# A decoder layer in five stages: loads and constants of each stage taken in the stage ahead, and the mixer's round in another order

## What is computed

```python
x = layernorm(x + mixer(x))                     # Mamba-2 block
x = layernorm(x + cross_attention(x, ctx, ctx)) # 16 heads of 64, softmax over 77 keys
x = layernorm(x + experts(x))                   # top 2 of 8, each with its own layernorm
```

## Time and profile before

| what | value |
|---|---|
| median of 3 runs | 2413.42 us |
| profiled execution, its own time | 2424.2 us |
| its span, first to last instruction | 2422.4 us |
| TensorE busy | 2166.8 us, 89% |
| VectorE busy | 1706.4 us, 70% |
| ScalarE busy | 1502.7 us, 62% |
| GpSimd busy | 1158.3 us, 48% |
| mean granted TensorE clock | 0.935 |

### The profile page before, as it was taken

How to read it: one execution, slowest core, us unless ns; L and a number is a source line. 1 busy time by engine, 2 the same in 40 slices (tenths; PEclk the granted TensorE clock), 3 DMA queues, 4 the chain that set the end, 5 groups by cost and what they waited for, 6 DMA issues and landing times. The chain is left out here.

```text
span 2422.4 us, 53619 instructions
## 1 busy us (share of the span) xinstructions
PE 2166.8 (89%) x15740; PEld 1925.9 (80%) x15741; DVE 1706.4 (70%) x4406; ACT 1502.7 (62%) x3174; POOL 1158.3 (48%) x1379
## 2 busy tenths in 40 slices
PE   5999999999995988999999999999949999999776
PEld 5888888878885977888888888888848998999633
DVE  5777777777775325677767767776738777777778
ACT  5777777777773426666666666666615565655433
POOL 2556556556553002334434434343336676766655
PEclk8999999999996999999999999999969999999955
DMA  4111111111101552232222223222167777777488
GB/s 145 32 35 35 35 35 35 35 35 35 35 30 39 188 189 73 89 105 79 82 91 78 82 78 95 77 82 90 52 193 222 230 237 229 232 237 228 144 294 266
DMA packets 185344, 278.70 MB, mean 115 GB/s; under 512 B 26092, under 2 KB 107508, under 8 KB 185268
## 3 DMA queue, kind: packets, MB, share of 16 engines
q1 hardware_dynamic: 171220, 241.04, 32.2%
q0 software_dynamic: 12960, 35.67, 4.1%
q10 hardware_dynamic: 1088, 1.07, 0.2%
HBM read 184.33 MB, written 93.38 MB: 115 GB/s over the span
## 5 line engine op out<-in xcount | busy, mean ns | idle before, releaser
L1499 ACT ACTIVATE b_wk_f<-b_ps_s,b_nmx 128x77 f32<-128x77 f32 x1024 | 233.7, 347 | 15.4 <-DVE b_nmx L1547 15.4
L599 DVE SCALAR_TENSOR_TENSOR a_conv<-a_xc_pad,a_cw,a_conv 128x256 f32<-128x256 f32 x384 | 217.9, 628 | 10.7 <-ACT a_conv L478 10.7
L1507 ACT ACTIVATE b_pT<-b_ps_pT 77x1024 f32<-77x1024 f32 x128 | 130.6, 1020 | 142.5 <-PE b_ps_pT L1405 142.5
L112 PE MATMUL c_ps_h<-c_xT_hi,c_w 128*128 128x256 f32 x568 | 168.0, 296 | 36.4 <-DMA c_b_c<-in_c_b 26.9
L2114 POOL DMA_INDIRECT made_scratch<-c_o_s,c_to x142 | 150.5, 1060 | 98.7 <-issue 40.5
L1986 ACT ACTIVATE c_hid<-c_ps_h,c_b_c 128x256 f32<-128x256 f32 x284 | 111.1, 474 | 119.7 <-issue 71.9
L1563 DVE TENSOR_TENSOR b_oT_lo<-b_ps_oT,b_oT_hi 128x512 fp32r<-128x512 f32 x128 | 88.0, 687 | 130.1 <-ACT b_oT_hi L1513 130.1
L1490 ACT ACTIVATE b_qT<-b_ps_q,b_bq_s 128x256 f32<-128x256 f32 x256 | 107.5, 472 | 113.2 <-PE b_ps_q L114 111.1
L1792 POOL CAST w<-b_w_raw 128x256 f32 (+1 forms) x32 | 13.6, 426 | 324.9 <-DMA b_w_raw<-in_c_w 324.9
L112 PE MATMUL c_ps_o<-w,c_h_hi 128*128 x568 | 161.3, 284 | 6.6 <-DVE c_h_lo L2030 6.6
L2030 DVE TENSOR_TENSOR c_h_lo<-c_hid,c_h_hi 128x1024 fp32r<-128x1024 f32 x71 | 98.0, 1380 | 97.9 <-ACT c_h_hi L1995 66.5
(11 more groups left out here) (286 smaller groups left out, 7822.5 us busy)
## 6 DMA issues: line engine op xcount, KB each, us to landing
c_w<-parts_scratch SPq DMA_DIRECT2D x71, 1024.0 KB
c_xa<-sent_scratch SPq DMA_DIRECT2D x71, 260.0 KB, 2.9
d_got<-made_scratch SPq DMA_DIRECT2D x32, 512.0 KB, 5.2
keys_scratch<-k_k_s SPq DMA_DIRECT2D x8, 1232.0 KB, 4.7
b_kz<-keys_scratch SPq DMA_DIRECT2D x64, 154.0 KB, 2.8
b_vv<-values_scratch SPq DMA_DIRECT2D x32, 308.0 KB
a_xT_f<-in_xT SPq DMA_DIRECT2D x32, 256.0 KB, 3.0
a_x_f<-in_x SPq DMA_DIRECT2D x32, 256.0 KB, 2.7
```

Of the source, the lines that this page charges most:

```text
L112: eng.matmul(out, lh, rh, start=start, stop=False)
L599: dve.scalar_tensor_tensor(out=conv[:, m, :], in0=xc_pad[:, m, k:k + L], scalar=cw[:, m, k:k + 1], in1=conv[:, m, :], op0=ALU.mult, op1=AL ...
L1499: last = act.activation(pe_[:, u.par, c, :], s_scores[:, c // (C // GM), c % (C // GM), :], ACT.Exp, bias=nmx[:, u.par, c:c + 1])
L1507: act.activation(pT[:, u.par, :, :], ps_pT[0:LK, :, :], ACT.Copy).then_inc(s_pTc, 1)
```

## The change

The mixer's lists are put in another order on four engines. On TensorE `turn_x` comes first, `cumulate` behind `turn_y`, `step_size` between the halves of `decay`, and `out` behind `in_z`. On ScalarE `take_x` and `x_high_next` stand ahead of `cum_high`, `take_bc` behind both exponentials and `squares` behind `silu_z`. On VectorE `normalise` stands first and the taps follow both `weigh` steps. On GpSimd `scale_x` stands ahead of `inv_rms`.

`prep_decay` and its waits move ahead of VectorE's rounds; the first `x_low` moves ahead of GpSimd's wait for the constants. The attention weights are loaded in round 1, together with the first context chunk, by a new `KeysHead`. The key weights are split in the mixer's last rounds (`keys_high`, `keys_low`). The mixer no longer waits for its last stores; the keys stage does, on ScalarE and SyncE. The context has one raw buffer instead of two. The keys stage loads attention's first x1 and keys for two items. To make room several tiles become views of others (the mixer's split weights lie in the key weights' place, `mk_pair` in `e_x`, `wo_stage` in `mt`, the attention stage's small tiles in `c_f`, `mk` and the split weights).

```diff
         w_stage = sb("w_stage", [P, KD, W_IN])
-        w_hi = sb("w_hi", [P, KD, C_DT], F32R)
-        w_lo = sb("w_lo", [P, KD, C_DT], F32R)
-        wo_stage = sb("wo_stage", [P, MI, D])
+        w_hi, w_lo = following.wk_hi, following.wk_lo
...
+            def load_following(b):
+                if b.known() and b.value() == 1:
+                    following.load(sp)
+
             load_xT(Item(0, 1))
-            following.load(sp)
-            run_steps(sp, n_seq, [(store, 3), (load_xT_ahead, 0), (load_x, 0)], spare=2)
-            for par in (0, 1):
-                sp.wait_ge(s_x1_out[par], 16 * (n_seq // 2))
+            run_steps(sp, n_seq, [(store, 3), (load_xT_ahead, 0), (load_x, 0), (load_following, 0)], spare=2)
...
             run_steps(pe, n_seq, [
-                (in_x, 0), (cumulate, 1), (turn_y, 2), (turn_x, 1), (in_bc, 0), (scores, 1), (decay(0), 1),
-                (out, 2), (decay(1), 1), (in_z, 0), (step_size, 0), (mix, 1), (mix_off, 1)])
+                (turn_x, 1), (in_x, 0), (turn_y, 2), (cumulate, 1), (in_bc, 0), (scores, 1), (decay(0), 1),
+                (step_size, 0), (decay(1), 1), (in_z, 0), (out, 2), (mix, 1), (mix_off, 1)])
...
             run_steps(act, n_seq, [
-                (cum_high, 1), (x_high_next, 0), (y_high, 2), (take_xc, 0), (take_bc, 0), (exp_rc, 1),
-                (exp_decay(0), 1), (take_x, 1), (squares, 2), (exp_decay(1), 1), (silu_z, 0), (silu_conv, 0),
+                (keys_high, 2), (x_high_next, 0), (take_x, 1), (cum_high, 1), (y_high, 2), (take_xc, 0), (exp_rc, 1),
+                (exp_decay(0), 1), (exp_decay(1), 1), (take_bc, 0), (silu_z, 0), (squares, 2), (silu_conv, 0),
                 (softplus, 0)], spare=2)
...
             run_steps(dve, n_seq, [
-                (cum_parts, 1), (y_low, 2), (mask_g, 1), (normalise, 3), (taps(0, 1), 0), (weigh(0), 1),
-                (taps(1, 2), 0), (weigh(1), 1), (taps(2, 3), 0), (bias_dt, 0), (add_d, 1), (prep_once, 0),
+                (keys_low, 2), (normalise, 3), (cum_parts, 1), (y_low, 2), (mask_g, 1), (taps(0, 1), 0), (weigh(0), 1),
+                (weigh(1), 1), (taps(1, 2), 0), (taps(2, 3), 0), (bias_dt, 0), (add_d, 1), (prep_once, 0),
                 (residual, 2), (log_decay, 0)], spare=2)
...
+            x_low(Item(0, 0))
             pool.wait_ge(s_load, 16 * N_LOADS)
             pool.wait_ge(s_pow, 4)
-            x_low(Item(0, 0))
...
             run_steps(pool, n_seq, [
-                (x_low_next, 0), (spread_cum, 1), (inv_rms, 2), (scale_x, 1), (join, 1), (inv_std, 2)], spare=2)
+                (x_low_next, 0), (spread_cum, 1), (scale_x, 1), (inv_rms, 2), (join, 1), (inv_std, 2)], spare=2)
...
+class KeysHead:
...
+    def load(self, sp):
+        self.weights.load(sp)
+        sp.dma_start(self.c_f[:, :, :], self.ctxT[:, :, 0:self.ROWS]).then_inc(self.s_c_in[0], 16)
+
+    def high(self, act):
+        act.wait_ge(self.weights.s_c, 16 * self.weights.CONSTANTS)
+        act.activation(self.wk_hi[:, :, 0:self.weights.DH], self.weights.wk_f[:, :, :], ACT.Copy).then_inc(self.s_khi, 1)
+
+    def low(self, dve):
+        dve.wait_ge(self.s_khi, 1)
+        dve.tensor_tensor(self.wk_lo[:, :, 0:self.weights.DH], self.weights.wk_f[:, :, :],
+                          self.wk_hi[:, :, 0:self.weights.DH].bitcast(F32), ALU.subtract).then_inc(self.s_klo, 1)
...
             def load_c(ch):
-                if ch >= 2:
-                    sp.wait_ge(s_chi, ch - 1)
-                    sp.wait_ge(s_clo, ch - 1)
-                sp.dma_start(c_f[:, ch % 2, :, :], ctxT[:, :, ROWS * ch:ROWS * ch + ROWS]).then_inc(s_c_in[ch % 2], 16)
+                sp.wait_ge(s_chi, ch)
+                sp.wait_ge(s_clo, ch)
+                sp.dma_start(c_f[:, :, :], head.ctxT[:, :, ROWS * ch:ROWS * ch + ROWS]
+                             ).then_inc(s_c_in[ch % 2], 16)
...
-            load_c(0)
             load_c(1)
             for ch in range(CHUNKS):
                 for sub in range(SUBS):
...
+                if ch == CHUNKS - 2:
+                    for par in (0, 1):
+                        sp.wait_ge(head.s_x1_out[par], 16 * (n_seq // 2))
+                    proj.load_xa(sp, x1)
+                    sp.wait_ge(s_ready, 2)
+                    sp.wait_ge(s_k_out[0], 16)
+                    proj.load_keys(sp, keys)
```

More of the change, by code:

```diff
@@ L941, in load, with __init__, sb @@
         sp.dma_start(self.mk[:, :, :], masks).then_inc(self.s_c, 16)
+class KeysHead:
+    ROWS = 8 * 77
+    def __init__(self, nc, ctx, signals, weights, ctxT):
+        def sb(name, shape, dt=F32):
+            return ctx.enter_context(nc.sbuf_tensor("k_" + name, shape, dt))
+        self.weights, self.ctxT = weights, ctxT
+        self.wk_hi = sb("wk_hi", [P, KD, 1152], F32R)
+        self.wk_lo = sb("wk_lo", [P, KD, 1152], F32R)
+        self.c_f = sb("c_f0", [P, KD, self.ROWS])
+        self.s_c_in, self.s_x1_out = ([signals.take(f"k_{n}{i}") for i in range(2)] for n in ("c_in", "x1_out"))
+        self.s_khi, self.s_klo = (signals.take("k_" + n) for n in ("khi", "klo"))
+    def load(self, sp):
[8 more added lines that the diff above has]
+                          self.wk_hi[:, :, 0:self.weights.DH].bitcast(F32), ALU.subtract).then_inc(self.s_klo, 1)
 class Projections:
@@ L959, in __init__, with load_xa, load_keys, keys_values_phase @@
         self.kz = sb("kz", [P, 2, 2, self.MH, self.LK])
-def keys_values_phase(nc, n_seq, signals, done_with, ctxT, weights, proj, w2, routing, keys, values):
+        self.xa = sb("xa", [P, 2, NT, D])
+        self.s_xa_in, self.s_kz_in = ([signals.take(f"b_{n}{i}") for i in range(2)] for n in ("xa_in", "kz_in"))
+    def load_xa(self, sp, x1):
+        sp.dma_start(self.xa[:, 0, :, :], x1[0:L, :].rearrange("(c p) d -> p c d", p=P)).then_inc(self.s_xa_in[0], 16)
+    def load_keys(self, sp, keys):
+        for b in range(2):
+            for a in range(2):
+                half = slice(self.HD * a, self.HD * a + self.HD)
+                sp.dma_start(self.kz[half, b, a, :, :].rearrange("p m k -> p (m k)"), keys[b, half, :]
+                             ).then_inc(self.s_kz_in[b], 16)
+def keys_values_phase(nc, n_seq, signals, done_with, head, weights, proj, w2, routing, keys, values, x1):
     LK, HD, DH, MH = proj.LK, proj.HD, proj.DH, proj.MH
@@ L1003, in keys_values_phase @@
         s_w, s_c = weights.s_w, weights.s_c
[L1004 to L1008, removed]
+        s_c_in, s_klo = head.s_c_in, head.s_klo
+        s_k_out, s_v_out = ([sem(f"{n}{i}") for i in range(2)] for n in ("k_out", "v_out"))
+        s_k, s_v, s_kc, s_vc, s_chi, s_clo, s_vhi, s_vlo, s_ohi, s_ready = (
+            sem(n) for n in ("k", "v", "kc", "vc", "chi", "clo", "vhi", "vlo", "ohi", "ready"))
+        w_stage = weights.w_stage
         block = ctx.enter_context(nc.Block())
@@ L1095, in _ @@
                         act.wait_ge(s_k_out[i % 2], 16 * (i // 2))
+                    if i == 0:
+                        for par in (0, 1):
+                            act.wait_ge(head.s_x1_out[par], 16 * (n_seq // 2))
                     for m in range(MH):
@@ L1142, in _, with attention_phase @@
             done_with.clear(pool)
-def attention_phase(nc, n_seq, signals, x1, keys, values, x2, weights, proj, w2, rows_in, routing):
+def attention_phase(nc, n_seq, signals, x1, keys, values, x2, weights, head, proj, w2, rows_in, routing):
     LK, HD, DH, MH = proj.LK, proj.HD, proj.DH, proj.MH
@@ L1301, in load_keys @@
             def load_keys(b):
-                if not b.before(2):
-                    sp.wait_ge(s_s, b.ago(2).count(4, 4))
+                if b.before(2):
+                    return
+                sp.wait_ge(s_s, b.ago(2).count(4, 4))
                 for a in range(2):
@@ L1308, in load_keys, with load_values_next @@
                                  ).then_inc(s_kz_in[b.par], 16)
+            def load_values_next(b):
+                if not b.before(1):
+                    load_values(b)
             def load_values(b):
```

92 lines of the change are left out of this document (46 added, 46 removed).

## The result

| | before | after |
|---|---|---|
| median | 2414.1 us (2406.55 to 2420.32) | 2465.87 us (2460.42 to 2477.26) |
| span of the profiled execution | 2422.4 us | 2475.4 us |
| mixer, spacing of items 2 to 31 | 22.74 us | 24.97 us |
| granted clock, 400 to 600 us | 0.95 | 0.84 |

The median before is now that of four runs. The changed kernel is slower, by about 2%: ratio 1.0223, 95% interval 1.0199 to 1.0247, about +52 us by the medians. The forecast was 2434 us with a range of 2390 to 2460. The direction was right, the time lies above the range.

What follows compares the result with a forecast made beforehand. The prediction took the order of the mixer's round to decide, through ScalarE's chain and TensorE's clock. Rounds of 23.85 us give +33, seams −12, so +21 on 2413.4: 2434 us, range 2390 to 2460.

Steps and rivals of the forecast that it cites:

- ScalarE's chain up to `decay(1)`: Mixer round: ScalarE's work from `cumulate` through `exp_decay(0)` takes 6.8 us, ends at 12.0, and `decay(1)` starts then.
- What TensorE owes behind it: Mixer round: TensorE's work from `decay(1)` to the round's end, 10.2 us, making 22.15 us at full clock.
- The wait for the logs and the one for B and C: Mixer, TensorE: waits of 0.99 us before `cumulate` and 0.26 us before `out` would be gone.
- the term of the clock: Mixer: a low-clock spell in practically every round, on `in_z` and `out`, loses 1.7 us a round; bounds 0 and 2.7.
- (c): Mixer: a spell begins within the wait and holds through `out`, or inputs come late; 24.6 us rounds, 2457 us; chance 0.10.
- Rival (b): Mixer: spells as often and costly as now, 6 rounds in 10 losing 1.7; 23.15 us rounds, 2413 us; chance 0.20.
- the sign that I named: Profile after, mixer: TensorE's `decay` waits for ScalarE's `e_x` in every round, up to 2 us.
- Rival (a): Mixer: the clock holds, rounds of 22.15 us or a little more, 2383 us in all; chance 0.15.
- The seams: Stage boundaries: start −6, mixer to keys −6, context buffer +2.5, keys to attention −2.7; together −12 us.
- the draining rounds: End of the mixer: its three draining rounds counted as 0, within 2 us.
- attention's opening: Keys to attention: x1 loaded before the stage opens saves 2.7 us; bounds −2 and −3.
- single context buffer: Keys stage: loads and value stores wait with one context buffer, +2.5 us over chunks 0 and 1; bounds 0 and +6.

Runs made afterwards that it cites:

- filler: Kernel after plus nine 512-column matmuls a mixer round, results unread, ahead of `scores`, `decay(0)` and `step_size`; 2374.47 us, ratio 0.9815.
- step_back: Kernel after with `step_size` moved behind `decay(1)` and `in_z` on TensorE; 2470.28 us, ratio 1.0214.
- best: Kernel after with `in_z` between the `decay` halves, `take_bc` between the exponentials, five dummy matmuls, context load behind the value stores; 2333.84 us, ratio 0.9651.
- order_only: Kernel before with only the four instruction lists of the mixer's round changed; 2478.77 us, ratio 1.0239.
- z_cover: Kernel after with `in_z` between `decay(0)` and `step_size` on TensorE, `take_bc` between the two exponentials on ScalarE; 2365.5 us, ratio 0.978.
- filler_last: Kernel after with only four dummy 512-column matmuls a round, ahead of `step_size`; 2467.4 us, ratio 1.0177.
- filler_first: Kernel after with only five dummy 512-column matmuls a round, two ahead of `scores`, three ahead of `decay(0)`; 2421.36 us, ratio 1.0025.

## Why the prediction missed

**The order of causes was right.** ScalarE's chain up to `decay(1)` sets the round once `out` is gone from between the halves. That chain was laid out to end 12.0 us after `turn_x` begins; in the kernel after it ends at 11.5 (420.10 to 431.59). What TensorE owes behind it was laid out as 10.2 and measures 10.68 at full clock (the next `turn_x` comes 0.92 after `mix_off` begins, not 0.52). The two errors cancel, which is luck: 22.15 forecast, 22.21 in `filler`. The wait for the logs and the one for B and C went.

**The step that failed is the term of the clock.** "I take 1.7" measured 2.8 a round (24.97 less 22.21), just above the forecast's own upper bound of 2.7. The mechanism was right, a spell in every round; its size was not. The forecast took the length of a spell from the present ones (they measure 3.4 us) and put it on `in_z` and `out`, where half of it is lost. Measured, the low clock lasts 8.0 us a round, in spells of 6.8 and 10.2. It begins in the waits and slows `step_size`, whose 0.8 us of delay is carried to `decay(1)`, and then `decay(1)` and `in_z`; `out` runs at full clock. About a third of it is lost, not half, since a part falls in waits. Of the rivals, (c) is the nearest, a spell that begins within the wait, 24.6 a round, with a chance of 0.10; measured 24.97. The rounds came to +65 instead of +33. Rival (b) was mispriced as well: "as costly as now" was put at 1.7 a spell, while the rounds that it was read from differ by 0.96 (23.11 less 22.15).

**Two waits were missed.** `scores` waits 0.54 us for `cum_parts`: the transposes that stood behind `cumulate` and hid this had moved ahead of it. And `step_size` was laid out directly behind `decay(0)`. It shares a PSUM bank with the row of `scores` that `exp_rc` reads, so it waits for `rc`, 0.5 to 1.1 us, which is ready only 0.9 us before the exponential of the first half. At full clock neither costs time (in `filler`, `decay(1)` comes 6.82 us after `cumulate`, and in step_back, with `step_size` out of the way, it does too); they lie in the stretch in which the clock falls. With the slow `step_size` in front of it, `decay(1)` never waited for `e_x`, so the sign that I named did not appear.

**Rival (a) has no support here.** The page TensorE: Matmul & The Clock Gate of the Trainium skill (Part 1) ties the fall to an idle stretch longer than any single wait of this round; by it the round would have been 22.15. The runs disagree with that rule: in the kernel after, the longest wait of the mixer's rounds from 100 to 700 us is 1.1 us and the clock falls in every round from 100 to 640, and it stays up when the same waits are filled.

**The seams were right, term by term, but for the draining rounds.** Start −7.2 (forecast −6), mixer to keys −6.5 (−6), attention's opening 7.33 to 4.55, −2.8 (−2.7), single context buffer +3.7 (the stage's +0.9 with that 2.8 added back; forecast +2.5, bound 6; best shows that the load ahead of the stores is what holds them). Together −12.8 against −12. The draining rounds, counted as 0 within 2, cost 3.6; this belongs to the order, as order_only, with the old stages, loses 3.8 from item 31's copy to the first key tile.

Still open: whether it is the pauses or the thin matmuls between them (`scores`, `step_size`) that bring the clock down. Every filler closed a pause and made the stretch denser at once. The waits before `scores` and `decay(0)` are not enough by themselves: z_cover keeps both, with `in_z` behind them, and has a spell in only 9 of 29 rounds.

## What to carry over

An instruction list in fixed order needs, between a result and its consumer, work that waits for nothing. Before moving such a cover, name what takes its place, and look up every tile that the substitute shares: `step_size` shared a bank with the very chain it was to cover, and `in_z` is a good cover only once `take_x` is early. Where TensorE's work is thin and broken by several short waits, price the lower clock over the whole spell, waits and small steps included, and try useful dense work there, or, failing that, matmuls for nothing: here nine of them gave back 2.8 us a round.

## What the runs showed of the hardware

- The granted clock fell to 0.50 with no single wait above 1.1 us. In the round of 24.9 us, TensorE had waited 0.54 and 0.75 us and the first 0.2 us of a third wait since `cumulate`, 5.0 us earlier, and had run matmuls of 8 to 512 columns in between. In the other two kinds of round it fell already in the second wait.
- Once down, it stays down although TensorE is busy without a gap: spells of 6.8 and 10.2 us in the kernel after, 3.4 to 10.2 us in filler_last, 3.4 us in filler_first and in the kernel before (all from 100 to 640 us). In the round of 24.9 us it came back in the middle of `in_z`, after 5.9 us without a gap.
- Small matmuls feel it as well: `step_size`, 8 matmuls of 8 columns, takes 0.95 to 1.06 us at full clock and 1.88 at half.
- Nine matmuls of 512 columns, some 2.1 us of TensorE's time (0.23 us from one to the next, as in `in_z`), made the round 2.76 us shorter (24.97 to 22.21).
